# Expert blocks: weights from a stock in SBUF, copied by VectorE, in place of one load from HBM per block

## The reference, cut to what matters

```
def _moe(x, Wg, W1, b1, W2, b2):          # layer 1, inside _L1_ffn_ref
    logits = xf @ Wg.T
    idx = jnp.argmax(logits, axis=-1)     # one of 8 experts for a row
    for e in range(E):
        m = (idx == e)[:, None].astype(xf.dtype)
        h = jax.nn.relu(xf @ W1[e] + b1[e])           # 128 -> 512
        out = out + m * (h @ W2[e] + b2[e])           # 512 -> 128

def _L2_ffn_ref(x, gate_w, expert_bias, w_up, w_down):   # layer 2
    ...
    top_w, top_i = jax.lax.top_k(weights, K)          # two of 8 experts for a row
    for e in range(E):
        h = jax.nn.gelu(jnp.einsum('bsh,ih->bsi', x, w_up[e]), approximate=False)
        y = jnp.einsum('bsi,hi->bsh', h, w_down[e])
        out = out + sparse_w[..., e:e + 1] * y
```

## Time and profile before

| | us |
|---|---|
| median of 3 runs (2859.16 to 2870.3) | 2863.14 |
| the profiled execution, own time | 2859.45 |
| its span, first to last instruction | 2857.6 |
| blocks of layer 1, from the first turn to the last | 1349.33 to 1433.41 |
| blocks of layer 2, from the first turn to the last | 2177.86 to 2330.29 |

### The profile page before, as it was taken

How to read it: one execution, slowest core, us unless ns; L and a number is a source line. 1 busy time by engine, 2 the same in 40 slices (tenths; PEclk the granted TensorE clock), 3 DMA queues, 4 the chain that set the end, 5 groups by cost and what they waited for, 6 DMA issues and landing times. The chain is left out here.

```text
span 2857.6 us, 48988 instructions
## 1 busy us (share of the span) xinstructions
PE 2198.9 (77%) x17390; PEld 1124.5 (39%) x17406; DVE 1960.6 (69%) x3720; ACT 1534.3 (54%) x3059; POOL 1225.7 (43%) x1274
## 2 busy tenths in 40 slices
PE   6999988886899895663937877887524967888886
PEld 2333334554444443553822333332224862333332
DVE  7888867675657662663269999999662228888894
ACT  4788872122566662331547777776311225777775
POOL 5524203332434311342456777777573435433310
PEclk9999997887999997776978999999757988999998
DMA  4121220000111112012930000000015961123110
GB/s 119 27 44 27 43 67 1 1 1 1 37 41 44 38 32 60 23 23 77 321 116 0 1 0 1 1 0 1 5 44 180 302 221 24 32 48 56 34 31 16
DMA packets 127626, 152.81 MB, mean 53 GB/s; under 512 B 19992, under 2 KB 108760, under 8 KB 126776
## 3 DMA queue, kind: packets, MB, share of 16 engines
q1 hardware_dynamic: 120792, 136.12, 17.6%
q0 software_dynamic: 6592, 13.56, 1.4%
HBM read 96.15 MB, written 25.59 MB: 43 GB/s over the span
## 5 line engine op out<-in xcount | busy, mean ns | idle before, releaser
L479 DVE TENSOR_REDUCE a_mx<-banks 128x2 f32<-128x1024 f32 (+3 forms) x768 | 805.3, 1087 | 230.4 <-PE banks L1051 125.4
L892 ACT ACTIVATE a_prob<-banks 128x512 f32<-128x512 f32 (+3 forms) x1536 | 744.8, 541 | 264.5 <-PE banks L1089 145.8
L1116 PE MATMUL banks<-a_prob,a_vaug 128*32 128x256 f32 (+2 forms) x5632 | 432.5, 388 | 0.2
L2234 POOL TENSOR_TENSOR m_hc<-m_h,m_cs 128x512 f32<-128x512 f32 x256 | 332.2, 1322 | 111.2 <-DVE m_h L2090 105.4
L1089 PE MATMUL banks<-a_Qs,a_Ks 64*128 64x512 bf16 (+3 forms) x1536 | 322.9, 362 | 46.3 <-DMA a_Qs<-a_negm 23.4
L1042 PE MATMUL banks<-a_Ks,a_Qs 63*128 63x512 bf16 (+3 forms) x1536 | 283.8, 366 | 37.9 <-DVE a_mx L479 30.1
L2090 DVE TENSOR_TENSOR_SCAN m_h<-banks,m_u 128x512 f32<-128x512 f32 x256 | 300.0, 1206 | 16.1 <-issue 12.8
L2389 PE MATMUL banks<-m_hc,kc 128*128 128x512 f32 x512 | 281.7, 634 | 14.6 <-POOL m_hc L2234 8.3
L2296 ACT ACTIVATE banks<-m_dt,acoef 128x512 f32<-128x512 f32 x256 | 174.6, 688 | 119.8 <-DVE m_h L2090 119.4
L1042 PEld LDWEIGHTS banks<-a_Ks,a_Qs 63*128 63x128 bf16 x1536 | 74.2, 93 | 329.3 <-issue 165.4
L1116 PEld LDWEIGHTS banks<-a_prob,a_vaug 128*32 128x32 f32 x5632 | 118.8, 109 | 155.0 <-issue 115.0
(11 more groups left out here) (438 smaller groups left out, 4229.2 us busy)
## 6 DMA issues: line engine op xcount, KB each, us to landing
c_wbuf<-in_w2e SPq DMA_DIRECT2D x71, 512.0 KB
b_wbuf<-in_w1e SPq DMA_DIRECT2D x39, 578.0 KB
a_Ks<-a_parts SPq DMA_DIRECT2D x252, 64.0 KB
a_Qs<-a_parts SPq DMA_DIRECT2D x252, 64.0 KB
rows_in<-in_unused SPq DMA_DIRECT2D x1, 4579.5 KB, 18.5
c_yb<-rows_in SPq DMA_DIRECT2D x71, 64.5 KB
a_mixed_in<-rows_back SPq DMA_DIRECT2D x16, 256.0 KB, 4.4
a_Qs<-a_negm SPq DMA_DIRECT2D x192, 2.0 KB
```

Source lines behind the costliest of these rows:

```text
L479: dve.tensor_reduce(both[:, :, c], m_bank(u)[:, :, 0:keys[c % NT]], AX.X, ALU.max).then_inc(S("m_read"), 1)
L892: act.activation(prob[:, n % DEEP, first_query[kt]:T], s_bank(u)[:, first_query[kt]:T], ACT.Exp, scale=scale).then_inc(S("s_read"), 1)
L1116: i = pe.matmul(V[32 * hl:32 * hl + 32, q0:q1], vaug[:, b % 3, kt, g % NG * GH + hl, :], prob[:, (4 * a + hl) % DEEP, q0:q1], start=kt == ...
L2234: gp.tensor_tensor(hc[:, n % 6, :], h[:, n % 4, :], cs[:, k % 4, :], ALU.mult).then_inc(S("weighed"), 1)
```

## The change

The weights of all eight experts are loaded once into a tensor `stock` in SBUF, by eight DMAs that SyncE issues in the stage in front: in `units_all` behind the 64 loads of its input, in `route_all` as SyncE's only work. In `blocks_all` SyncE loads only the rows. VectorE gets a new piece, `vector_weights`: for each block it loads the column where the expert's weights start into a register and copies the 1156 or 1024 columns from `stock` to `wbuf`. It is due at `at(j)` - 6, and from block 6 on it waits until block j - 6 is evicted, since `wbuf` now has 6 places in place of 8. TensorE's up(j) waits for the copy in addition. The table `starts` holds columns in place of rows. The buffer `weights` is made earlier, with no other effect.

```diff
+        def load_stock(sp, stock, w_rows):
+            columns = w_rows.shape[1]
+            for e in range(E8):
+                stocked.add(sp.dma_start(stock[:, e * columns:(e + 1) * columns], w_rows[e * P:(e + 1) * P, :]))
...
-                RING = 8
-                wbuf, yb, yT = room("wbuf", [P, RING, columns]), room("yb", [P, RING, ROW]), room("yT", [P, 3, P])
+                RING, HELD = 8, 6
+                wbuf = room("wbuf", [P, HELD, columns])
+                yb, yT = room("yb", [P, RING, ROW]), room("yT", [P, 3, P])
...
+                def vector_weights(dve):
+                    for j in range(blocks):
+                        yield at(j) - 6.0
+                        if j == 0:
+                            dve.wait_ge(S("starts"), 1)
+                            dve.wait_ge(stocked.sem, all_stocked)
+                        if j >= HELD:
+                            dve.wait_ge(S("evicted"), j - HELD + 1)
+                        w0 = nc.values_load(starts[0:1, 1, j:j + 1], engines=[dve.engine], min_val=0, max_val=(E8 - 1) * columns,
+                                            skip_runtime_bounds_check_because="clamped to the last expert")
+                        dve.tensor_copy(wbuf[:, j % HELD, :], stock[:, bass.ds(w0, columns)]).then_inc(S("chosen"), 1)
...
-                        w0 = nc.values_load(starts[0:1, 1, j:j + 1], engines=[sp.engine], min_val=0, max_val=(E8 - 1) * P,
-                                            skip_runtime_bounds_check_because="clamped to the last expert")
-                        sp.dma_start(wbuf[:, j % RING, :], w_rows[bass.ds(w0, P), :]).then_inc(S("loaded_%d" % (j % RING)), 16)
...
-                        pe.wait_ge(S("loaded_%d" % (j % RING)), 32 * (j // RING + 1))
+                        pe.wait_ge(S("loaded_%d" % (j % RING)), 16 * (j // RING + 1))
...
                         pe.wait_ge(S("yT"), j + 1)
+                        pe.wait_ge(S("chosen"), j + 1)
...
+                def sync_stock(sp):
+                    yield 0.0
+                    load_stock(sp, *later)
```

More of the change, by code:

```diff
@@ L1492, in unit_rows, with units_all @@
             return [(xall[s * 16:(s + 1) * 16, n, :, 0:C], v[s, :, n, :, :]) for s in range(SB)]
-        def units_all(x_view, hold_view, wb, run):
+        def units_all(x_view, hold_view, wb, run, later):
             with ExitStack() as ctx:
@@ L1841, in units_all, with blocks_all @@
                 run_lanes(all_lanes)
-        def blocks_all(tag, blocks, func, w_rows, run, bias):
+        def load_stock(sp, stock, w_rows):
+            columns = w_rows.shape[1]
+            for e in range(E8):
+                stocked.add(sp.dma_start(stock[:, e * columns:(e + 1) * columns], w_rows[e * P:(e + 1) * P, :]))
+        def blocks_all(tag, blocks, func, stock, run, bias):
             columns = 2 * FF + (NF + C if bias else 0)
@@ L1859, in blocks_all @@
                 used, sent = {}, {}
-                behind = [t.n for t in back]
+                behind, all_stocked = [t.n for t in back], stocked.n
                 def S(name):
@@ L1894, in vector_starts @@
                     link(dve, dve.tensor_reduce(ex, past, AX.X, ALU.add))
-                    link(dve, dve.tensor_scalar(low, ex, E8 - 1.0, float(P), ALU.min, ALU.mult))
+                    link(dve, dve.tensor_scalar(low, ex, E8 - 1.0, float(columns), ALU.min, ALU.mult))
                     dve.tensor_copy(starts[:, 1], low).then_inc(S("starts"), 1)
@@ L1966, in tensor_downs @@
                             i = pe.matmul(D[:, j % 2, 0:C], hb[:, j % 3, f * P:(f + 1) * P],
-                                          wbuf[:, j % RING, FF + f * C:FF + (f + 1) * C], start=f == 0, stop=f == NF - 1)
+                                          wbuf[:, j % HELD, FF + f * C:FF + (f + 1) * C], start=f == 0, stop=f == NF - 1)
                         i.then_inc(S("down"), 1)
@@ L1997, in vector_out @@
                         if bias:
-                            i = dve.tensor_tensor(ob[:, j % 4, :], D[:, j % 2, 0:C], wbuf[:, j % RING, 2 * FF + NF:columns],
+                            i = dve.tensor_tensor(ob[:, j % 4, :], D[:, j % 2, 0:C], wbuf[:, j % HELD, 2 * FF + NF:columns],
                                                   ALU.add)
@@ L2022, in build @@
             load_weights([(w_b, pb)], [(w_c, pc)])
-            units_all(x1, x2, wb, run_counts[:, 0])
-            blocks_all("b_", BLOCKS_1, ACT.Relu, w1e, run_counts[:, 0], True)
+            stock = sb(ctx, "stock_b", [P, E8 * w1e.shape[1]])
+            units_all(x1, x2, wb, run_counts[:, 0], (stock, w1e))
+            blocks_all("b_", BLOCKS_1, ACT.Relu, stock, run_counts[:, 0], True)
         def mamba_all(xres, wc, wconv, acoef, views, later):
@@ L2465, in mamba_all, with route_all @@
                 run_lanes(all_lanes)
-        def route_all(xres, w, weights, run):
+        def route_all(xres, w, weights, run, later):
             with ExitStack() as ctx:
@@ L2632, in all_lanes @@
                     if name == "sync":
-                        return []
+                        return [sync_stock(eng)]
                     own = [vector_set(eng)] if name == "vector" else []
@@ L2647, in build @@
             out_b = out.rearrange("(b t p) c -> p b t c", b=B, p=P)
+            weights = sb(ctx, "weights", [P, B, 2, NT])
             mamba_all(xres, wc, wc("convr"), acoef, views, (w_d, pd))
-            weights = sb(ctx, "weights", [P, B, 2, NT])
-            route_all(xres, wd, weights, run_counts[:, 1])
-            blocks_all("c_", BLOCKS_2, ACT.Gelu, w2e, run_counts[:, 1], False)
+            with ExitStack() as inner:
+                stock = sb(inner, "stock_c", [P, E8 * w2e.shape[1]])
+                route_all(xres, wd, weights, run_counts[:, 1], (stock, w2e))
+                blocks_all("c_", BLOCKS_2, ACT.Gelu, stock, run_counts[:, 1], False)
             c3 = wd("cols3")
```

7 lines of the change are left out of this document (4 added, 3 removed).

## The result

The changed kernel takes 2834.02 us in the median (2825.57 to 2836.17), the kernel before on the same chip 2866.58 (2859.16 to 2870.3). The ratio is 0.9875, with a 95% interval of 0.9858 to 0.9891: faster by 1.25%. The range 2831 to 2877 holds the time, but the mechanism that was called the likeliest is not the one that happened.

A forecast was written before the change was run, and what follows sets the result against it. The DMA engines were taken to bound the two block stages; 15.5 us from steady blocks plus 2.0 us from the starts gave 17.5 us off the 2863.14 us median, so 2846 us, range 2831 to 2877.

The forecast's parts named there:

- The bound: Block stages: DMA engines set the mean period, TensorE's own is 1.90 us; at most 28.0 us to gain in blocks.
- The copy's price: VectorE's copy of a block's weights within SBUF: 0.76 us for 1156 columns, 0.69 for 1024.
- The PSUM row: Rival price for VectorE's copy, at PSUM's rate: 1.36 and 1.22 us; 2877 or 2869; slow copy or slow load, chance 0.20.
- The register load: VectorE, between ob and the copy: 0.45 us taken in series, ends 0.27 and 0.9.
- what costs nothing: Covered work: stock's DMAs, longer indirect DMAs, and the copy's wait for ob(j-5) or earlier, already in front on VectorE.
- The loop: VectorE-TensorE chain over two periods, 4.08 us in layer 1, 4.01 in layer 2; gain 15.5 us; chance 0.52.
- The first rival: Blocks: VectorE hidden, load and copy under 0.96 us, period 1.90, gain 30 us, 2833 us; chance 0.15.
- The starts: Block stages' starts: first rows no longer behind weight loads, 1.4 and 0.6 us off, 2.0 us together.
- The stock: Stages in front: eight DMAs, 4.7 MB in layer 1, 15 us, start in SyncE's gap and cost nothing.
- The lock: Blocks: rival that VectorE's copy and GpSimd's indirect DMA exclude each other, 2885 us, chance 0.13; expected the copy holds GpSimd off.
- The slow rival: Blocks: the indirect DMA holds VectorE's copy for all its 0.96 us, loss 21.7 us, 2885 us; chance 0.13.
- The signs: Expected in the trace: turns 2.0 us apart, DMA share under 0.2, up(j) waiting for yT by 0.1 us.

The follow-up runs named there:

- no_weights: Kernel before, with weights loaded only for the first eight blocks of each layer (output not the reference's): 2838.64 us, 0.9902 of the kernel before.
- dma_stock: Changed kernel, but SyncE's DMAs copy each block's weights from the stock in SBUF, eight places, no VectorE copy: 2876.65 us, 1.0063 of the kernel before.
- held5: Changed kernel with five places for the weights in place of six: 2842.68 us, 0.9909 of the kernel before.
- late_stock: Changed kernel with the stock loaded at the beginning of each block stage, not in the stage in front: 2844.69 us, 0.9902 of the kernel before.
- before3: Kernel before, unedited, timed again with a trace on the same chip as the changed kernel: 2870.39 us, 0.9996 of its twin.
- again3: Changed kernel, unedited, timed again with a trace on the chip of the kernel before: 2833.26 us, 0.9872 of the kernel before.
- after_yT: Changed kernel with VectorE's copy due 1.5 us later, behind yT instead of in front: 2827.28 us, 0.9882 of the kernel before.

## Why the prediction was right and wrong

**The bound, right.** The DMA engines set the pace, the undisturbed period is 1.90 us, and 28.0 us was the most that the blocks could give. `no_weights` shows it from the side of before, `dma_stock` shows that the engines' work and not the source is what costs. One number on the way was off, with no effect on the sum: 658 thousand bytes in 2.170 us are 303 GB/s, not 310.

**The copy's price, right.** 0.76 and 0.69 us from the two SBUF rows; 0.764 and 0.694 measured. The PSUM row was the wrong neighbour, as the text chose.

**The register load, right by itself, wrong in its place.** This is the step that failed. The load alone is 0.304 us, but the sum took 0.45 in series between `ob` and the copy, plus 0.03. What passes there is 0.15. The error came in with the change's own section and was repeated under what costs nothing: that the copy has "a wait for VectorE's own last instruction", `ob(j-5)` ("or earlier", the prediction adds, without following it up). The code says `j - HELD + 1`, and with HELD = 6 this is a count that `ob(j-6)` raises. Then nothing holds the register load back, and it runs under `ob`, as the load at 1393.3 does. A smaller part: yT begins 0.10 us before the copy's end (1394.39 against 1394.49). The loop is 4.08 - 0.48 + 0.15 - 0.10 = 3.65 us over two periods, 1.83 each, less than TensorE's 1.90, so the term of 12.5 us (28.0 - 15.5) is zero. `held5` puts the wait where the prediction had it and gets 3.98 us (1.90 + 2.08), against the 4.08 predicted for it; the 0.10 less is yT's early start, and the gap of 0.47 us bears out the 0.48 for load and handing over.

The first rival, VectorE hidden with the gain 28.0 + 2.0 = 30 us, is what happened: the block stages are 30.4 us shorter. Its condition was written down rightly, load and copy under 0.96 us. Measured is 0.15 + 0.76 = 0.91. It got a chance of 0.15, since SyncE's gap of 0.48 us was taken for VectorE's, and the count of the semaphore, read wrongly, gave no reason to expect an overlap. That the range holds the measured time is owed to this rival's 2833 and not to the loop, whose band ended at 2838.

**The starts, right in size.** 2.0 us predicted, 1.7 + 0.9 = 2.6 measured.

**The stock, right.** `late_stock` prices the cover at 9.5 us in the block stages. The two stages in front are as long with the load as without: 236.1 us for units in `before3` and in `again3`, and 122.1 and 122.2 us from the routing stage's first instruction to `ends`.

**The lock, its order wrong.** The prediction had the copy begin 0.2 us behind the indirect DMA's start and hold it off. In the changed kernel the copy starts first (1393.72 against 1393.84), since its load is hidden, and GpSimd's DMA takes 0.51 us longer, hidden under a period of 1.90. The Trainium skill, "SBUF — State Buffer", section "Who interferes with whom", lets the first of the two hold for its whole instruction. Where GpSimd is first the trace doesn't agree: in `held5` a copy begun 0.20 us after a DMA's start takes its 0.77 us. The Trainium skill says on the same page, in "A bandwidth-pool intuition that's wrong (but worth ruling out)", that a DMA that is held stays blocked until about 115 ns behind the end of VectorE's instruction. A DMA that ends 0.12 us behind its copy fits it, and that is so where the DMA began first and the copy held it: the one at 1393.71 in `after_yT` (1395.06 and 1394.94). Where the copy began first, the DMA ends 0.82 us behind it (1395.31 and 1394.49). The slow rival needed a DMA that holds the copy for its whole length, and neither the changed kernel, where the copy is first, nor `held5`, where the DMA is, has one.

**The signs.** Turns 1.90 apart and not 2.0, no wait of up for yT, DMA share 0.24 and 0.26 where under 0.2 was said. The rows cost the DMA engines more for a byte than the weights did: 0.24 of the time for 67 GB/s, against 0.94 for 319 in the earlier trace rows.

## What to carry to other kernels

Before a register load and its wait are put in series with the instruction in front, count the semaphore: whether it is raised by that very instruction or by an older one decides. One buffer less put the load's length back between `ob` and the copy (0.47 us for 0.15), 7.6 us in all here. Where DMA engines are the bound, an engine with idle time can move the data inside SBUF; here that took 31 us off the block stages, while DMAs that did it from SBUF gained nothing. Price the loop with and without each overlap before calling one of the two the likeliest, if they lie on two sides of the next bound.

## What the runs showed of the hardware

- VectorE's register load (0.304 us, 0.55 at most) begins while the instruction ahead still computes, if its wait allows it: it starts at 1393.3 where `ob` runs from 1393.27 to 1393.56, with 0.15 us between `ob` and the copy; where it has to wait for `ob`, 0.47 us.
- A copy of fp32 within SBUF and GpSimd's indirect DMA exclude each other over part of the DMA only. In `after_yT`, a copy begun up to 0.50 us after the DMA's start runs undisturbed and the DMA is held (1.35 us in place of 0.95); in layer 2 of the same trace one begun 0.51 us after it takes 0.94 us in place of 0.69, one begun 0.65 us after it 0.80, and the DMA its 0.96.
- DMAs of 512 and 578 KB from SBUF to SBUF moved 276 and 305 GB/s, no more than those from HBM to SBUF (300 and 319).
